# Two stages of a two-layer block: turning all batches' rows at the start of retention, and time mixing with one variance, a shifted view and split products

## What is computed

```
# retention, layer 0, on z = layernorm(x)
qkvg = z @ w_attn                      # 16 query heads, 8 key and 8 value heads of 64, 8 gates
s = rope(q) . rope(k) / 8
a = exp(2 log|s| + G_t - G_s), causal, divided by its largest of the row   # G: running sum of log gates
y = (a @ v) / sum(a), standardised per head, times ln_w
x = x + y @ w_proj

# time mixing, layer 1, on z = layernorm(x)
xn = (z - mean(z)) * rsqrt(var(z) + 1e-5) * ln_w + ln_b
prev = xn one step earlier in time (0 at the start)
xk, xv, xr = xn * tm + prev * (1 - tm)         # with three vectors tmk, tmv, tmr
S_t = sigmoid(decay_w) * S_(t-1) + (xk @ Wk.T)_t * (xv @ Wv.T)_t
x = x + z + sigmoid(xr @ Wr.T) * (S @ Wo.T)
```

## Time and profile before

| | |
|---|---|
| median of 3 runs | 2386.46 us (2384.07 to 2386.97) |
| the profiled execution | 2385.33 us, its span 2383.6 us |
| TensorE busy | 2137.9 us, 90% |
| VectorE busy | 1397.9 us, 59% |
| ScalarE busy | 1343.4 us, 56% |
| GpSimd busy | 352.0 us, 15% |
| mean granted TensorE clock | 0.950 |

### The profile page before, as it was taken

One profiled execution on the slowest core, in us unless ns is written; L12 is line 12 of the kernel. 1 busy time (PEld: TensorE's weight loads), 2 busy tenths in 40 slices (PEclk: granted clock), 3 DMA queues, 4 the chain that ended last, 5 costly groups with the idle time before them and its releaser, 6 DMA issues. The chain is left out here.

```text
span 2383.6 us, 37629 instructions
## 1 busy us (share of the span) xinstructions
PE 2137.9 (90%) x14685; PEld 1627.4 (68%) x14685; DVE 1397.9 (59%) x2352; ACT 1343.4 (56%) x2571; POOL 352.0 (15%) x302
## 2 busy tenths in 40 slices
PE   6999999999967977699999879999999999666797
PEld 4777777787735546588888646887787877433575
DVE  4455455454536653499999744445454545464587
ACT  2566566565634423488888525665665656402574
POOL 3111112121110000300000121121121211102501
PEclk9999999999988988899999879999999999877899
DMA  4000001010021003799999530010101010013786
GB/s 150 19 32 24 28 28 37 19 37 19 1 96 79 1 1 126 287 355 361 360 362 357 178 137 19 19 36 19 37 19 36 19 37 1 1 71 124 304 338 235
DMA packets 53727, 262.58 MB, mean 110 GB/s; under 512 B 9512, under 2 KB 9896, under 8 KB 26672
## 3 DMA queue, kind: packets, MB, share of 16 engines
q1 hardware_dynamic: 47104, 244.71, 27.5%
q0 software_dynamic: 2560, 8.39, 1.1%
q10 hardware_dynamic: 3888, 7.08, 0.8%
HBM read 243.91 MB, written 16.25 MB: 109 GB/s over the span
## 5 line engine op out<-in xcount | busy, mean ns | idle before, releaser
L508 DVE COPY c_pt<-bank 128x512 f32<-128x512 f32 x256 | 177.1, 692 | 549.4 <-PE bank L342 549.3
L658 ACT ACTIVATE c_pr<-wide,c_nmax 128x512 f32<-128x512 f32 x512 | 349.3, 697 | 165.5 <-DVE c_nmax L500 84.0
L231 POOL TENSOR_TENSOR c_clo<-c_raw,c_chi 128x512 fp32r<-128x512 f32 x128 | 167.5, 1313 | 1008.0 <-ACT c_chi L635 1008.0
L342 PE MATMUL bank<-ident,c_pr 128*128 128x128 f32 x2048 | 268.2, 273 | 13.0 <-DVE c_pt L508 10.2
L342 PEld LDWEIGHTS bank<-ident,c_pr 128*128 128x128 f32 x2048 | 237.6, 140 | 49.2 <-DVE c_pt L508 12.4
L92 PE MATMUL bank<-c_wv_hi,c_chi 128*128 128x512 f32 x512 | 217.6, 425 | 20.0 <-POOL c_clo L231 18.6
L1656 DVE TENSOR_TENSOR moe_wlo<-moe_raw,moe_whi 128x2048 fp32r<-128x2048 f32 x97 | 219.2, 2286 | 19.7 <-ACT moe_whi L1516 19.6
L643 ACT ACTIVATE c_khi<-bank,c_cols 128x512 fp32r<-128x512 f32 x128 | 88.1, 688 | 252.3 <-PE bank L94 252.3
L92 PE MATMUL bank<-c_chi,c_wk_hi 128*128 128x512 f32 x512 | 213.7, 417 | 9.2 <-ACT c_v L649 9.1
L94 PE MATMUL bank<-c_wv_hi,c_clo 128*128 128x512 f32 x512 | 202.4, 395 | 0.0
L93 PE MATMUL bank<-c_wv_lo,c_chi 128*128 128x512 f32 x512 | 202.2, 395 | 0.0
(11 more groups left out here) (355 smaller groups left out, 4029.6 us busy)
## 6 DMA issues: line engine op xcount, KB each, us to landing
moe_hr<-in_L_ffn_w SPq DMA_DIRECT2D x68, 1024.0 KB, 6.9
moe_raw<-in_L_ffn_w SPq DMA_DIRECT2D x52, 1024.0 KB, 7.0
c_raw<-in_ctx SPq DMA_DIRECT2D x32, 1024.0 KB, 4.9
moe_raw<-in_L_ffn_we_gate SPq DMA_DIRECT2D x15, 1024.0 KB, 7.1
moe_raw<-in_L_ffn_we_up SPq DMA_DIRECT2D x15, 1024.0 KB, 5.8
moe_raw<-in_L_ffn_we_down SPq DMA_DIRECT2D x15, 1024.0 KB, 6.1
slot_outputs<-moe_ob ACTq DMA_DIRECT2D x27, 256.0 KB, 7.0
ret_w<-in_L_attn_w_attn SPq DMA_DIRECT2D x4, 1024.0 KB, 9.0
```

Of the source, the lines that this page charges most:

```text
L231: nc.gpsimd.tensor_tensor(clo[:, g % 2, c, :], raw[:, c, :], f32(chi[:, g % 2, c, :]), ALU.subtract) \
L342: last = pe.transpose(TB[n % 2][:, h * P:(h + 1) * P], pr[:, u % 2, h, n * P:(n + 1) * P], k["ident"][:])
L508: nc.vector.tensor_copy(pt[:, n, :], TB[0][:]).then_inc(pt_dve, 1)
L658: nc.scalar.activation(pr[:, u % 2, h, :], S[h][:], ACT.Exp, bias=nmax[:, b % 2, i, at:at + 1], scale=-1.0 if masked else 1.0, accum_out=d ...
```

## The change

Retention: `xn` and `xT` get a slice for each batch. VectorE normalises all four batches before anything else; TensorE turns batch 0, projects it, and then turns batches 1 to 3, each into a bank of its own of the four that the scores use later; ScalarE copies them behind batch 0's projection. The scores of each batch wait once for all four copies. Nothing of it is left in the loop.

Time mixing: z's variance isn't measured again. With v the variance of x, z has v / (v + e), and so zn = (x - mean) * rsqrt(v (1 + e) + e * e); both roots are taken in one instruction, zn is made first, and z only at the end, where it is added. TensorE turns zn batch by batch into four banks, and ScalarE scales and shifts out of PSUM into `zT`, whose rows have 129 places, the first of them zero. So the earlier time step is a view of the same tile, moved by one place: `rise` = now - earlier, once, and each mix is rise * tm + earlier, one instruction. The mixed tiles, the weights and the state are each split in a high part (ScalarE rounds to fp32r) and a low part (VectorE subtracts), and TensorE multiplies with `three_products`, chunk by chunk as they come. The weights come through two raw tiles, the first transfer of the stage is Wv, ahead of the six small columns, and the last two wait until a raw tile has been read. The scans run batch by batch, and so do their split and the output.

```diff
@@ stage_retention
-        xn = m.sb("xn", [P, D])
-        xT = m.sb("xT", [P, C, P])
+        xn = m.sb("xn", [P, NB, D])
+        xT = m.sb("xT", [P, NB, C, P])
...
                 def turn_x(b):
                     pe.wait_ge(S["xn"], b + 1)
-                    after(pe, S["qk_copied"], 4 * b)
                     for c in range(C):
-                        last = pe.transpose(ps[4][:, c * P:(c + 1) * P], xn[:, c * P:(c + 1) * P], k["ident"][:])
+                        last = pe.transpose(ps[b][:, c * P:(c + 1) * P], xn[:, b, c * P:(c + 1) * P], k["ident"][:])
...
                     after(pe, S["num_read"], 4 * b)
+                    pe.wait_ge(S["xT"], NB)
...
                 project(0)
+                for b in range(1, NB):
+                    turn_x(b)
                 turn_qk(0)
                 sum_decay(0)
                 for b in range(NB):
-                    if b + 1 < NB:
-                        turn_x(b + 1)
                     scores(b)
...
                     keep_projection(0, g)
+                for b in range(1, NB):
+                    keep_xT(b)
                 gates(0)
...
                     more = b + 1 < NB
-                    if more:
-                        keep_xT(b + 1)
                     magnitudes(b)
...
-                normalise(0)
+                for b in range(NB):
+                    normalise(b)
                 dve.wait_ge(S["const_in"], 32)
                 rotate(0)
-                normalise(1)
...
-                    if b + 2 < NB:
-                        normalise(b + 2)
                     scale(b)
@@ stage_rwkv
+                sp.dma_start(raw[:, 0], weights[0]).then_inc(w_in[0], 16)
                 for i, n in enumerate(names):
                     sp.dma_start(cols[:, i, :], t["L1_attn_" + n]).then_inc(s_["c_in"], 16)
-                for i, n in enumerate(("Wv", "Wk", "Wr", "Wo")):
-                    sp.dma_start(w[i][:], t["L1_attn_" + n]).then_inc(s_["w_in"], 16)
+                sp.dma_start(raw[:, 1], weights[1]).then_inc(w_in[1], 16)
+                for i in (2, 3):
+                    sp.wait_ge(s_["wlo"], i - 1)
+                    sp.dma_start(raw[:, i % 2], weights[i]).then_inc(w_in[i], 16)
...
+                for i, (made, banks) in enumerate((("v_made", ps[4:8]), ("k_made", ps[0:4]))):
+                    pe.wait_ge(s_["wlo"], i + 1)
+                    for c in range(C):
+                        pe.wait_ge(s_["lo"], C * i + c + 1)
+                        for o in range(C):
+                            last = three_products(pe, banks[o][:], whi[i][:, c, o * P:(o + 1) * P], wlo[i][:, c, o * P:(o + 1) * P],
+                                                  flat(hi[i], c), flat(lo[i], c), c == 0, c == C - 1)
...
+                act.wait_ge(s_["var"], 1)
+                nc.scalar.sqrt(std[:], ve[:]).then_inc(s_["std"], 1)
+                high_weights(0)
                 act.wait_ge(s_["c_in"], 16 * len(names))
                 nc.scalar.activation(decay[:], cols[:, 5, :], ACT.Sigmoid).then_inc(s_["decay"], 1)
+                act.wait_ge(s_["rate"], 1)
+                for c in range(C):
+                    act.wait_ge(s_["turned"], c + 1)
+                    nc.scalar.activation(zT[:, c, :, 1:P + 1], ps[c][:].rearrange("p (b t) -> p b t", b=NB), ACT.Identity,
+                                         bias=cols[:, 1, c:c + 1], scale=cols[:, 0, c:c + 1]).then_inc(s_["zT"], 1)
+                for c in range(C):
+                    high(0, c)
+                high_weights(1)
+                for c in range(C):
+                    high(1, c)
+                high_weights(2)
...
+                def mix(i, c):
+                    dve.wait_ge(s_["rise"], c + 1)
+                    after(dve, s_["lo"], C * i + c - 1)
+                    nc.vector.scalar_tensor_tensor(out=blend[:, c % 2], in0=rise[:, c], scalar=cols[:, mix_col[i], c:c + 1],
+                                                   in1=zT[:, c, :, 0:P], op0=ALU.mult, op1=ALU.add).then_inc(s_["blend"], 1)
...
+                nc.vector.tensor_scalar(ve[:, 1, :], mv[:, :, 1], 1.0 + LN_EPS, LN_EPS * LN_EPS, ALU.mult, ALU.add) \
+                    .then_inc(s_["var"], 1)
...
+                for i in range(KINDS):
                     for c in range(C):
...
+                        if i == 0:
+                            dve.wait_ge(s_["zT"], c + 1)
+                            nc.vector.tensor_tensor(rise[:, c], zT[:, c, :, 1:P + 1], zT[:, c, :, 0:P], ALU.subtract) \
+                                .then_inc(s_["rise"], 1)
+                        mix(i, c)
+                        if c > 0:
+                            low(i, c - 1)
+                    low(i, C - 1)
+                    low_weights(i + 1)
...
+                for b in range(NB):
+                    for o in range(C):
                         nc.vector.tensor_tensor_scan(state[:, o, b, :], rate[:, o, :], kv[:, o, b, :], 0.0, ALU.mult, ALU.add) \
                             .then_inc(s_["state"], 1)
+                    dve.wait_ge(s_["shi"], b + 1)
+                    nc.vector.tensor_tensor(slo[:, :, b, :], state[:, :, b, :], f32(shi[:, :, b, :]), ALU.subtract) \
+                        .then_inc(s_["slo"], 1)
+                for b in range(NB):
+                    s.mark(nc.vector.tensor_scalar(z[:, b, :], x[:, b, :], mv[:, b, 0:1], rstd[:, 0, b:b + 1],
+                                                   ALU.subtract, ALU.mult))
```

More of the change, by code:

```diff
@@ L1828, in stage_rwkv @@
         z, zn = m.sb("z", [P, NB, D]), m.sb("zn", [P, NB, D])
-        zT = m.sb("zT", [P, C, NB, P])
-        prev = m.sb("prev", [P, C, NB, P])
-        mixed = [m.sb(f"mixed{i}", [P, C, NB, P]) for i in range(3)]
-        w = [m.sb(f"w{i}", [P, C, D]) for i in range(4)]
+        zT = m.sb("zT", [P, C, NB, P + 1])
+        rise = m.sb("rise", [P, C, NB, P])
+        blend = m.sb("blend", [P, 2, NB, P])
+        hi, lo = ([m.sb(f"{n}{i}", [P, C, NB, P], F32R) for i in range(KINDS)] for n in ("hi", "lo"))
+        raw = m.sb("raw", [P, 2, C, D])
+        whi, wlo = ([m.sb(f"{n}{i}", [P, C, D], F32R) for i in range(KINDS + 1)] for n in ("whi", "wlo"))
         cols = m.sb("cols", [P, 6, C])
-        one_minus = m.sb("one_minus", [P, 3, C])
         decay = m.sb("decay", [P, C])
@@ L1880, in _, with flat @@
-                pe.wait_ge(s_["vT"], C)
-                pe.wait_ge(s_["mixed"], 3 * C)
+                def flat(tile, c):
+                    return tile[:, c].rearrange("p b t -> p (b t)")
                 for b in range(NB):
+                    pe.wait_ge(s_["zn"], b + 1)
                     for c in range(C):
-                        last = pe.matmul(ps[2 + b][:], mixed[2][:, c, b, :], w[2][:, c, :], start=(c == 0), stop=(c == C - 1))
+                        last = pe.transpose(ps[c][:, b * P:(b + 1) * P], zn[:, b, c * P:(c + 1) * P], k["ident"][:])
+                        if b == NB - 1:
+                            last.then_inc(s_["turned"], 1)
@@ L1894, in _, with high_weights, high @@
             def _(act):
-                for i in range(2):
-                    act.wait_ge(s_["var"], i + 1)
-                    nc.scalar.sqrt(std[:, i, :], ve[:, i, :]).then_inc(s_["std"], 1)
+                def high_weights(i):
+                    act.wait_ge(w_in[i], 16)
+                    nc.scalar.copy(whi[i][:], raw[:, i % 2]).then_inc(s_["whi"], 1)
+                def high(i, c):
+                    act.wait_ge(s_["blend"], C * i + c + 1)
+                    nc.scalar.copy(hi[i][:, c], blend[:, c % 2]).then_inc(s_["hi"], 1)
```

133 lines of the change are left out of this document (59 added, 74 removed).

## The result

| | before | after |
|---|---|---|
| median of the runs | 2386.7 us (2384.1 to 2389.1) | 2355.4 us (2352.2 to 2356.4) |
| ratio, 95% interval | | 0.9867 (0.985 to 0.9884) |
| profiled execution, its span | 2385.33, 2383.6 us | 2355.89, 2354.2 us |
| retention, first instruction to the next stage's first | 197.82 us | 187.79 us (-10.0) |
| time mixing, the same | 81.65 us | 63.19 us (-18.5) |

The forecast was 2355 us with 31.6 us gained, 13.5 in retention and 18.1 in time mixing. The total came out within a microsecond, its two terms did not: retention gave 3.5 us less, time mixing 0.4 more, and what lies outside both was 0.9 shorter, for which the change shows no reason: the experts stage behind time mixing was 4.0 us shorter, the first stage 2.2 longer, and both scatter like that between kernels that agree there (see Experiments).

The account below looks back on a forecast made before the run. TensorE is busiest, but in retention and time mixing something else ends last for 20 to 40 us each. 13.5 + 18.1 = 31.6 us off 2385.33 gives 2353.7, median 1.1 above: 2355 us; range 2347 to 2365.

Parts of the forecast that it names:

- Retention, batch 0: Moved transposes fill TensorE's idle gap before the rotated queries and the clock holds: gain 2.4 us.
- the cold value: Retention, batch 0, if the clock falls all the same: gain 0.5 us instead of 2.4.
- Batch 1: Retention: scores no longer wait for xn and run at full clock, 3.50 us instead of 6.51; gain 10.6 us.
- the clock stays low: Rival, 10%: batch 1's scores start earlier but at 1.2 GHz; retention gains 7.9 us instead of 13.5, total 2361 us.
- Batch 2: Retention: one set of transposes in a row of TensorE work costs 0.5 us.
- Clock levels elsewhere may fall otherwise: Later stretches begin at other moments, so their clock may differ: 3 us either way, two slow starts of 1.6 us.
- Time mixing up to the turned rows: Stage's start: zn starts where z did, transposes end at 2095.2 instead of 2102.3, first rise at 2096.3.
- The feeding chain: Time mixing on VectorE: from first rise to last sum 53.0 us, ending 2 us behind TensorE.
- rounding runs hand to hand: Rival, 13%: time mixing's low parts each wait for ScalarE's copy, 8.4 us more on VectorE; total 2363 us.
- Products 0.23 us apart: Time mixing on TensorE: one rounded product follows the next every 0.23 us, 44.2 us instead of 55.6.
- POOL's copy: Time mixing: POOL's copy of the decay slows a VectorE instruction beside it by 0.3 us.
- The other two rivals: Rounded product costs 0.869 us, 2473 us in all (2%); time taken away at xn and zn reappears there, 2384 us (5%).

Follow-up runs that it names:

- e5: Changed kernel plus 16 products with unread results in retention (4 in batch 0, 12 behind the last batch's scores): retention 184.16 us for 187.79, median 2353.3 us.
- e10: Changed kernel with the edits of e5 and e6 together: retention 183.75 us, time mixing 60.98 us, median 2351.6 us, ratio to before 0.986.
- e1: Changed kernel with time mixing of the kernel before: retention 187.40 us, time mixing 83.27 us, median 2374.4 us, ratio to before 0.9957.
- e3: Changed kernel with true float32 products in time mixing, no high and low parts: time mixing 69.36 us for 63.19, median 2357.0 us.
- e4: Changed kernel with the second normalisation worked out from its own statistics again: time mixing 66.25 us for 63.19, median 2359.2 us.
- e8: Changed kernel with time mixing's six small column transfers issued ahead of Wv: time mixing 66.11 us for 63.19, median 2356.5 us.
- e9: Changed kernel with one of the three products left out throughout time mixing: time mixing 63.12 us for 63.19, median 2355.6 us.
- e6: Changed kernel with the low parts of the k, r and output weights moved later on VectorE: time mixing 60.86 us for 63.19, median 2352.2 us.
- e7: Changed kernel with retention's normalisations up front, but transposes of x and their copies left in the loop: retention 190.62 us for 187.79, median 2358.1 us.
- e11: e10 plus five more float32 products with unread results in time mixing: time mixing 60.58 us for 60.98, median 2351.2 us.

## Why the prediction was right in sum and wrong in two terms

- **Retention, batch 0** failed: 2.4 us were taken, the cold value 0.5 stood beside it, 0.05 came. The step that fell is "With the idle cut from 5.5 to 3.9 us I take it that the clock holds". The idle time was about right (4.13), the level was not: the clock fell at the same moment of the stage as without the transposes, only 2.9 us behind them instead of the 4.2 us of idleness before. Four products in the gap make the difference (e5). e10 has them too, and its stage opened like that of the kernel before (full clock from 9.8 us on); there the scores start 32.5 us into the stage for 34.95, the 2.4 us of the forecast. The Trainium skill (TensorE: Matmul & The Clock Gate, section What's actually happening) has the throttled level as the default, which activity releases. The traces of after and of e5 agree with that; whether the transposes were too few, or the idleness behind them too long, they don't tell apart.
- Even the 0.5 us did not come in this profile: the full clock of the stage's start came 0.45 us later (10.2 us into the stage for 9.8), so all behind it ran 0.3 us later, and the sums took 2.91 us for 2.84. In e1, e3, e4 and e8, with the same retention and the full clock from 9.7 or 9.8 us on, batch 0's scores start 34.5 to 34.6 us into the stage for 34.95: there it came.
- **Batch 1** held: -11.0 for -10.6, by the steps named. The scores ran at the full clock, 3.47 us. The rival "the clock stays low" is out; the weighing ran on VectorE, and `rotate(2)` waited only for the gates.
- **Batch 2** held (0.5). **The last batch** was not in the sum: 1.5 us given back, since the same 12.00 and 3.46 us of idleness met the falls and rises of the clock at other moments of the work. "Clock levels elsewhere may fall otherwise", with 3 us either way, covers its size but not its place; e5 shows the cause. Retention's term was over by 3.5 us: 2.35 in batch 0 and 1.5 in the tail, less the 0.4 that batch 1 gave beyond its term. The clock in the gap and in the tail took 3.6 us, which e5 gave back.
- **Time mixing up to the turned rows** held: the rise at 9.12 us for 9.5. The columns landed in time, the 3 us set aside for them were not needed; e8 shows what the order they stand in saves.
- **The feeding chain** held within half a microsecond (last sum 62.3 for 62.8), and so did "VectorE is last, by 2 us": e9 and e6 show that it was so, and that taking two of the three waits away is worth 2.3 us. The chain of the forecast had these waits (1.2 us each). The 12 waits of the rival "rounding runs hand to hand" did not come; the rounded copies were there when a low part began, or came within 0.1 us, except for the weights and for the states, whose 0.7 us the forecast had. TensorE's last product ended 49.3 us behind the first `rise`; the forecast wrote 49.7, though its own terms (3.5, 1.6 and 44.2) add up to 49.3.
- **Products 0.23 us apart** held: 0.227.
- **POOL's copy**: 0.3 us foreseen, 0.36 came (1.04 us for 0.68), on the first `rise` and not on the low part, where the forecast looked for it. The Trainium skill (SBUF — State Buffer, section Who interferes with whom) speaks of an exclusive lock. The trace goes with that in its order: the low part, which had begun first, lost nothing (2.29 us), the copy took 1.21 us where it takes 0.61 in e3, and the `rise`, which began during the copy, lost 0.36.
- **The other two rivals** are out: a rounded product costs 0.227 us and not 0.869, and what was taken away at `xn` and at zn did not come back elsewhere in either stage, but for the 1.5 us of the tail.
- **The sum**: the profiled execution gained 29.4 us for 31.6 (3.5 less in retention, 0.4 more in time mixing, 0.9 outside), and the median, set 1.1 above the profiled execution, came out 0.4 under it. So a miss of 2.2 us became one of 0.6. That is luck, of a size that the range allowed for.

## What to carry to other kernels

Sum up stage by stage and judge stage by stage: a program whose last stage scatters by 8 us hides a repair of 2 us, while the stage's own length repeats mostly to 0.1 to 0.7 us, and at worst here to 1.6, where the clock rose later. A gapless engine need not be the one that ends a stage; look at whose last instructions start on results that lie ready, then at that engine's short waits, which can often be filled with its own later work. And where a step is moved for one engine's sake, follow its copy on the other engine: in retention that copy, stuck behind a root that waited for VectorE, weighed more, as the rows of e7 read, than the transposes. And a little work in a gap need not hold the clock: twelve transposes here did not.

## What the runs showed of the hardware

- Twelve transposes of 128x128 that end 4.13 us before the next work did not keep TensorE's clock at 2.4 GHz (it fell to 1.2 at 727.5, 2.9 us after they ended, and stayed for 6.9 us). It fell 26.8 to 27.5 us into the stage in seven profiles with them and at 26.8 or 26.9 in three without. With four float32 products of 128x512 behind them it held (e5, e10, e11).
- The same instructions with the same waits take 0.7 us more or less by the moment at which the clock rises again (after, 859.26: 4.34 us; before, 868.46: 3.68). In e1 the unchanged time mixing ran 1.6 us longer for it.
- VectorE's sum of 512 columns beside POOL's copy of 512: 1.04 us for 0.68, and the copy 1.21 for 0.61 (e3). In e4 the copy lay beside the low part of the weights, which had begun first: the copy 1.46 us, the low part 2.28 as ever.
- At the full clock one rounded product of 128x512 follows another every 0.227 us (after), 0.68 for three, where a true float32 one takes 0.86 (e3).
